# Cross-attention and mixture of experts on one core: fill and gates reordered, probabilities of a pair's second batch transposed a slot later

## What is computed

```python
x = x + tanh(g_xattn) * (softmax(rms(LN(x) @ Wq) . rms(ctx @ Wk)) @ (ctx @ Wv) @ Wfc + b)   # 4 heads of 64
n = LN(x)                                     # per token
w, e = softmax(top2(n @ Wr.T))                # 8 experts, 2 a token
keep = position_in_expert(e) < CAP            # 97 tokens of a batch for each expert
x = x + tanh(g_ffn) * sum_k w_k * keep_k * (n @ We[e_k])
```

## Time and profile before

| | |
|---|---|
| median of 3 runs | 1402.53 us (1402.27 to 1404.48) |
| the profiled execution | 1401.25 us, of which the traced span 1399.5 us |
| PE busy | 1372.1 us (98%) |
| PEld / DVE / ACT / POOL busy | 81% / 73% / 65% / 55% |
| first slot of the first step (its `ctx_transpose`) | 75.66 us after the span's start |
| TensorE clock in the 40 slices of the page | 9 tenths or more throughout |

### The profile page before, as it was taken

How to read it: one execution, slowest core, us unless ns; L and a number is a source line. 1 busy time by engine, 2 the same in 40 slices (tenths; PEclk the granted TensorE clock), 3 DMA queues, 4 the chain that set the end, 5 groups by cost and what they waited for, 6 DMA issues and landing times. The chain is left out here.

```text
span 1399.5 us, 26935 instructions
## 1 busy us (share of the span) xinstructions
PE 1372.1 (98%) x8142; PEld 1140.4 (81%) x8142; DVE 1020.8 (73%) x3057; ACT 910.5 (65%) x2600; POOL 775.1 (55%) x947
## 2 busy tenths in 40 slices
PE   7799999999999999999999999999999999999998
PEld 6688888888888888888888888888888888888876
DVE  5777777777777777777777777777777777767763
ACT  6666667766667756667666667666677666676652
POOL 3345555565566565556565555565555555565644
PEclk9999999999999999999999999999999999999999
DMA  5001010111010111110111110110101110101000
GB/s 162 29 18 45 30 43 18 44 45 45 28 44 18 45 45 37 36 45 18 45 45 34 39 34 28 45 44 31 42 25 38 45 45 28 45 18 45 25 16 23
DMA packets 70289, 53.72 MB, mean 38 GB/s; under 512 B 45888, under 2 KB 53504, under 8 KB 70144
## 3 DMA queue, kind: packets, MB, share of 16 engines
q1 hardware_dynamic: 70144, 52.00, 12.1%
HBM read 25.11 MB, written 16.78 MB: 30 GB/s over the span
## 5 line engine op out<-in xcount | busy, mean ns | idle before, releaser
L332 PE MATMUL bkM<-we,x2T 128*128 128x512 f32 x3072 | 792.6, 401 | 3.5 <-DVE we L855 2.7
L332 PEld LDWEIGHTS bkM<-we,x2T 128*128 128x128 f32 x3072 | 554.7, 188 | 130.4 <-ACT a_out L684 8.4
L684 ACT ACTIVATE a_out<-bkM,gate 128x256 f32<-128x256 f32 x512 | 217.0, 482 | 190.9 <-PE bkM L332 189.8
L1067 DVE SCALAR_TENSOR_TENSOR acc_v<-bkM,gate,acc_v 128x256 f32<-128x256 f32 x384 | 184.8, 481 | 106.2 <-PE bkM L332 90.5
L498 POOL TENSOR_TENSOR a_sum<-a_sum,a_out 128x256 f32<-128x256 f32 x256 | 189.1, 739 | 56.8 <-ACT a_out L684 20.6
L485 POOL TENSOR_TENSOR probs<-probs,p_inv 128x308 f32<-128x308 f32 x128 | 89.7, 702 | 214.8 <-DVE p_inv L960 214.8
L453 POOL TENSOR_TENSOR rstd<-ve,minus_half 128x4 f32<-128x4 f32 x64 | 65.2, 1019 | 149.1 <-DVE ve L872 148.9
L453 POOL TENSOR_TENSOR q_r<-q_ve,minus_half 128x8 f32<-128x8 f32 x64 | 105.1, 1644 | 48.6 <-DVE q_ve L945 48.6
L590 ACT ACTIVATE xn<-x_sb,shift,rstd 128x256 f32<-128x256 f32 x128 | 66.5, 590 | 92.0 <-DVE shift L881 92.0
L453 POOL TENSOR_TENSOR k_r<-k_ve,minus_half 77x8 f32<-77x8 f32 x32 | 52.4, 1636 | 131.3 <-DVE k_ve L921 131.3
L503 POOL TENSOR_TENSOR y<-a_sum,acc_v 128x256 f32<-128x256 f32 x128 | 94.5, 739 | 17.3 <-issue 0.4
(11 more groups left out here) (178 smaller groups left out, 2727.3 us busy)
## 6 DMA issues: line engine op xcount, KB each, us to landing
x_sb<-in_x SPq DMA_DIRECT2D x32, 512.0 KB, 3.7
out<-y SPq DMA_DIRECT2D x64, 256.0 KB, 2.0
ctx_sb<-in_ctx SPq DMA_DIRECT2D x32, 154.0 KB
vf<-v_nat SPq DMA_DIRECT2D x64, 77.0 KB
stage<-in_L_ffn_We SPq DMA_DIRECT2D x2, 1024.0 KB, 6.2
vf<-v_nat SPq DMA_DIRECT2D x32, 52.0 KB
vf<-v_nat SPq DMA_DIRECT2D x32, 51.0 KB
vf<-v_nat SPq DMA_DIRECT2D x32, 26.0 KB
```

The lines of the kernel that those rows point to most:

```text
L332: mm = nc.tensor.matmul(out, l, r, start=(i == 0), stop=(i == len(terms) - 1))
L684: ins = nc.scalar.activation(a_out[:, t % 2, (e // 4) * 2 + i], bkM[1][:, i * D:(i + 1) * D], ACT.Copy, scale=gate[:, m.parity, t, e:e + 1])
L1067: nc.vector.scalar_tensor_tensor(out=acc_v[:, t], in0=bkM[0][:, i * D:(i + 1) * D], scalar=gate[:, m.parity, t, e:e + 1], in1=src, op0=ALU ...
```

## The change

On TensorE the transposes of the second batch's tiles (2 and 3) stand behind the chunk of slot 14 and ahead of the first batch's `attend`, and no longer in slot 13. On VectorE all of `gates(p)` goes from the head of slot 13 to slot 14, so behind the low parts of tiles 0 and 1. In the first round the matmuls on the identity are 17 instead of 30 and stand behind the context's transpose. In the second round ScalarE makes `ln2(p)` ahead of `k_part(f)`; VectorE makes the last four of `expert_lo` two by two earlier, and all of `row_max` ahead of `route(p, 0)`; TensorE makes all scores ahead of `logits_transpose`.

```diff
--- before.py
+++ after.py
@@ -793,9 +793,9 @@
                 weights_hi([FRONT_WEIGHTS, FRONT_WEIGHTS + 1])
                 q(f, 1)
                 q_part(f, 0)
+                ln2(p)
                 k_part(f)
                 q_part(f, 1)
-                ln2(p)
                 x2T_part(p, 0)
                 x2T_part(p, 1)
                 exps(f, 0)
@@ -1140,14 +1140,12 @@
                     chunk(k, m, p)
                     if f:
                         inverse(f, 3)
-                if k == 13:
+                if k == 13 and f:
+                    pT_part(f, 0)
+                    pT_part(f, 1)
+                if k == 14:
                     if p:
                         gates(p)
-                    if f:
-                        pT_part(f, 0)
-                        pT_part(f, 1)
-                if k == 14:
-                    if p:
                         kept_gates(p)
                     if f and f.n > 0:
                         pT_part(f, 2)
@@ -1195,19 +1193,19 @@
                 ln2_shift(p)
                 for ep in range(E // 2):
                     expert_lo(0, ep)
+                expert_lo(1, 0)
+                expert_lo(1, 1)
                 x2T_part(p, 0)
                 x2T_part(p, 1)
                 row_max(f, 0)
-                for ep in range(E // 2 - 1):
-                    expert_lo(1, ep)
-                row_max(f, 1)
+                expert_lo(1, 2)
+                expert_lo(1, 3)
+                for t in range(1, T):
+                    row_max(f, t)
+                inverse(f, 0)
                 route(p, 0)
-                row_max(f, 2)
-                inverse(f, 0)
-                row_max(f, 3)
-                expert_lo(1, E // 2 - 1)
+                inverse(f, 1)
                 route(p, 1)
-                inverse(f, 1)
                 inverse(f, 2)
                 inverse(f, 3)
                 gates(p)
@@ -1231,8 +1229,6 @@
         @block.tensor
         def _(pe):
             pe.wait_ge(const_ready, 4 + E + 3)
-            for _ in range(30):
-                pe.matmul(bkF[:, 0:P], ident[:], ident[:], start=True, stop=True)
 
             def moe(m, c):
                 t, ep = c // (E // 2), c % (E // 2)
@@ -1417,9 +1413,10 @@
                     if f:
                         p_transpose(f, 0)
                         p_transpose(f, 1)
+                if k == 14 and f:
+                    if f.n > 0:
                         p_transpose(f, 2)
                         p_transpose(f, 3)
-                if k == 14 and f:
                     attend(f, 0, 0, p)
                     attend(f, 1, 0, p)
                 if k == 15 and f:
@@ -1434,6 +1431,9 @@
             def first_round(f, g):
 
                 for k in range(SLOTS):
+                    if k == 1:
+                        for _ in range(17):
+                            pe.matmul(bkF[:, 0:P], ident[:], ident[:], start=True, stop=True)
                     if k == 2:
                         pe.wait_ge(stage_used, 1)
                         pe.wait_ge(setup_v, ZEROS)
@@ -1475,10 +1475,9 @@
                 x2_transpose(p, 1)
                 scores(f, 0)
                 logits(p)
-                scores(f, 1)
+                for t in range(1, T):
+                    scores(f, t)
                 logits_transpose(p)
-                scores(f, 2)
-                scores(f, 3)
                 moe(p, 0)
                 moe(p, 1)
                 for t in range(T):
```

## The result

The changed kernel takes 1390.59 us (median of 4 runs, 1390.25 to 1391.7), the kernel before in the same session 1402.4: a ratio of 0.9915 with the 95% interval 0.9898 to 0.9933. The direction was as predicted, the size only half: 11.8 us instead of 22.2, and the time lies 2.1 us above the range.

The account below looks back on a forecast made before the run. TensorE's queue was taken to bound the middle (busy 1257.52 of 1260 us), a chain over all engines the two rounds. 14.1 + 4.1 + 4.0 = 22.2 us off 1401.25 gives 1379.05, median 1380.3; range 1377 to 1388.5.

Parts of the forecast that it names:

- First round, 4.1 us: First round: ScalarE makes Wkv's high part at 8.1 instead of 12.17 us, moving the chain behind it 4.1 us earlier.
- One sign of being wrong: First round, TensorE: a lowered clock between 5 and 25 us would show the forecast wrong.
- The 0.148 us for a pass: First round: 60 identity passes in 8.86 us, so 34 take 5.0 us, hidden if they begin by 5.4.
- The lower bound, 0.7: First round: gain of only 0.7 us if TensorE falls to the half clock once, priced at 3.4 us.
- Second round, 4.0 us: Second round: earlier ln2, row maxima and first chunks bring the first attention forward; 4.0 us taken, bounds 1.3 to 4.7.
- The share of ln2: Second round: ScalarE's earlier ln2 brings x2T and the first exponentials 1.3 us forward, 58.25 to 56.95.
- both old waits go: Steps, TensorE: waits at bank E's transposes (0.16 us) and the first attention (0.19 plus 0.08 refill) both vanish.
- 30 x 0.47 = 14.1 us: Steps: 0.47 us gained in each of 30 steps, 14.1 us in all, bounds 12.9 to 14.4.
- The half microsecond of room: Steps, second attention: VectorE's low parts end at 706.72, the attention wants them at 707.25, so no new wait.
- Rival A: Steps: one more gate held by GpSimd, second attention waits 0.25 us, 7.5 us lost, 1387.8 us; chance 0.10.
- the refill that the forecast itself had counted at the first attention: Steps: 0.08 us by which the first attention lasts longer, read as TensorE's queue filling again after its wait.
- the end of the range: Upper end of the forecast time, from the rival with one more held gate: 1387.8, rounded to 1388.5 us.

Follow-up runs that it names:

- The run with short additions: Changed kernel with GpSimd's three additions for tile 2 in the steps on 16 columns instead of 256: 1380.5 us, ratio 0.9838.
- the run with split gates: Changed kernel with the first four gates back at the head of slot 13, the last two still in slot 14: 1380.29 us, ratio 0.9836.
- either move alone: Changed kernel with, in the steps, only VectorE's later gates (1390.38 us) or only TensorE's later transposes of tiles 2 and 3 (1394.65 us).
- VectorE's move alone: Changed kernel with TensorE's four transposes back in slot 13, so in the steps only VectorE's gates are later: 1390.38 us, ratio 0.9908.

## Why the prediction was half right

- **First round, 4.1 us:** measured 3.7, and 3.4 to 4.3 in the nine profiles with this first round. ScalarE's Wkv ran at 8.27 us instead of the 8.1 worked out from the load's landing: right. The layernorm was not done when Wkv's high part was (9.33): x landed later here, and ScalarE waited 0.37 us for it. One sign of being wrong did show, a lowered clock between 5 and 25 us: it rose at 9.96 us, where it rose at 6.69 before. The 0.148 us for a pass was a mean over both clocks, and the 34 passes took 6.5 us instead of 5.0. They were hidden with nothing to spare, as the first product could start at 10.8 and did at 10.85. The lower bound, 0.7, was far too low: 3.4 us at half the clock lose 1.7 us of a full queue's work and not 3.4, and in the two kernels in which the clock fell from 28.6 to 32.0 us the second context transpose stands at 35.58 and 35.73, against 34.80 to 35.01 in the six without such a fall and with an early rise.
- **Second round, 4.0 us:** measured 4.1, along the chain that was given: its sum put the first attention 27.8 us behind the round's start, and it stood at 28.2. That 4.0 and 4.1 agree is luck in part, since the nine profiles with this second round have 32.1 to 35.2 us for it (1.4 to 4.4 gained). The share of ln2 was off: in the new order the first exponentials come 1.0 us nearer to the round's start and not 1.3, since VectorE's six low parts take 4.53 us (six times 0.68 would be 4.1) beside GpSimd's additions of the bias and end only at 51.46, when x2T has been ready for 0.3 us. What the order of the low parts and row maxima gives by itself, and what the clock adds to it, these runs don't part.
- **Steps, both old waits go:** right; bank D to bank E is as worked out, and so is the first attention together with bank E's distance in front of it.
- **Steps, 30 x 0.47 = 14.1 us:** wrong, 3.2 us. The step that failed is "VectorE begins the gates at 703.77 and needs for them what it needed before, 703.74 - 701.97 = 1.77 us". They need 2.49 there. The start was right: den follows bank B's low part at once. But a duration was carried over from a place where two of the six were held behind GpSimd (w_top 0.49 us and the second g_part 0.71 as means over the steps) to one where three are (den 0.67, w_top 0.63, g_all 0.64). The half microsecond of room that the sum left was smaller than what one more such hold takes. The run with short additions shows that GpSimd's work is the cause, the run with split gates that the place of the chain is what counts.
- **Rival A was what happened**, mechanism and place: one more of the six held. The wait, 0.25 us predicted and 0.26 measured (0.25 as a mean over the steps), agrees by luck in part: the gates grew by 0.72 us and not 0.8, and the attention starts 0.10 behind the last low part, which the sum had at nothing. Its price, 7.5 us, left out the refill that the forecast itself had counted at the first attention: 0.25 + 0.09 = 0.34 a step makes 10.2 us, and 1380.3 + 10.2 = 1390.5, where 1390.59 was measured. With that price rival A's time, and so the end of the range, would have been 1390.5. That 0.1 us is left is luck: the old waits gave 0.45 a step and not 0.47, and the rounds 7.8 us and not 8.1, together 1.0 us less, while the median stands 0.3 us above the profiled execution and not 1.3. Its chance, 0.10, was too low: "GpSimd's work is the same" says nothing, as the gates had been moved from its gaps to under three of its instructions in a row.
- The forecast was about what the move can give: with the gates split a step takes 0.45 us less than before, and the kernel 1380.29 us (1378.87 to 1382.78). That the median meets the forecast to 0.01 us is luck.

The Trainium skill (SBUF — State Buffer, Who interferes with whom) lets only VectorE instructions with two inputs in SBUF, and forms such as tensor_scalar that may use two ports, be excluded by a GpSimd one. The trace agrees in both halves: den, a tensor_scalar with one input, is held (0.67 us against 0.14 before the change, where it ended before GpSimd's next instruction began), and the low parts, with one input in PSUM, take 0.55 us under GpSimd's additions as elsewhere. The prediction had read four gates out of that section; den is the fifth, and one of the two that were newly held.

## What to carry to other kernels

A duration belongs to the place in which it was measured: before moving a chain of small VectorE instructions, lay GpSimd's timeline beside the new place and count which of them, of the kinds that are held here, would start inside a GpSimd instruction, each at the price of the rest of that instruction. When two waits on a full engine are removed, look first at what the same supplier delivers last; here either move alone left the queue's end where it was, and of the reorderings tried only filling VectorE's idle 0.75 us with the head of the chain moved it. Price a new wait with its refill.

## What the runs showed of the hardware

- After a wait a run of twelve 256-column matmuls takes longer to the next start: the second attention 1.46 us instead of 1.37 (means over the steps, changed kernel and split gates), the first 1.47 instead of 1.40 behind a chunk (kernel before, and VectorE's move alone). So a wait cost TensorE 0.07 to 0.09 us beyond itself.
- The held gates end 0.02 to 0.05 us after the GpSimd instruction inside which they start: den at 695.12 and the addition at 695.10, w_top at 696.00 and 695.98, g_all at 696.90 and y at 696.86. The reciprocal, with one input, is not held: in the kernel before it starts at 702.15, inside GpSimd's scaling (702.14 for 0.70 us), and takes 0.18.
- The clock granted to TensorE in the rounds differs between kernels whose rounds are the same, and the rounds' length follows it. Where it was at 1.2 GHz for 3.4 us in all between its rise and the first step, that step began at 67.18 us (one kernel); for 6.8 us, at 67.83 to 68.81 (four); for 10.2 us, at 69.85 and 70.06 (two). With GpSimd's additions shortened in the steps alone it fell from 62.1 to 68.9 us. TensorE had idled 1.33 us before bank D's transposes and 0.82 in front of the first attention; in the changed kernel it idled 1.36 and 0.62 there, and the clock stayed up. The second round took 35.1 us in the one and 32.5 in the other. So the rounds' gain in one profile is known to some 3 us only, and their parts less well; the steps, at full clock throughout, repeat to 0.02 us (five kernels with the same steps).
